# Row maxima of attention from rounded q and k alone, two tiles of queries at once in the lower and upper 64 rows

## What is computed

```python
qkv = jnp.einsum('bte,fe->btf', x, Wqkv)          # split in q, k, v for 8 heads of 64
q = q + pe[None, None]
k = k + pe[None, None]
scores = jnp.einsum('bhtd,bhsd->bhts', q, k) / jnp.sqrt(jnp.asarray(D, q.dtype))
scores = jnp.where(causal[None, None], scores, jnp.asarray(-jnp.inf, q.dtype))
probs = jax.nn.softmax(scores, axis=-1)
attn = jnp.einsum('bhts,bhsd->bhtd', probs, v)
```

## Time and profile before

| | us |
|---|---|
| runs of the kernel | 678.23, 680.35, 681.81 (median 680.35) |
| span of the profiled execution | 680.5 |
| TensorE busy | 629.8 (93%) |
| VectorE busy | 513.4 (75%) |
| GpSimd busy | 505.5 (74%) |
| ScalarE busy | 442.2 (65%) |
| score pairs of the fifth head start at | 273.89 |
| score pairs of the sixth head start at | 330.62 |

### The profile page before, as it was taken

The page is one execution under the profiler, slowest core; times in us unless marked ns, Lnnn a source line. Parts: engine busy times, 40 slices in busy tenths (PEclk is TensorE's granted clock), DMA queues, the critical chain, the costliest instruction groups (busy, mean ns, idle before and its releaser), DMA issues. The chain is left out here.

```text
span 680.5 us, 9930 instructions
## 1 busy us (share of the span) xinstructions
PE 629.8 (93%) x3043; PEld 485.0 (71%) x3043; DVE 513.4 (75%) x1138; ACT 442.2 (65%) x617; POOL 505.5 (74%) x296
## 2 busy tenths in 40 slices
PE   5879999999999999999999999999966998989992
PEld 3647777777777777777777777777655896767761
DVE  3676888887977888888797788886778774785675
ACT  3536786676776668667677666867843666656671
POOL 8016898887888889898788888989986545466770
PEclk8988999999999999999999999999987998999997
DMA  7622322223322232222332223333000000000001
GB/s 200 140 47 48 79 62 47 47 47 70 71 47 46 48 78 63 48 47 47 69 71 47 47 48 70 70 88 116 0 1 0 2 1 1 0 17 0 15 0 31
DMA packets 29074, 33.72 MB, mean 50 GB/s; under 512 B 6977, under 2 KB 15970, under 8 KB 28898
## 3 DMA queue, kind: packets, MB, share of 16 engines
q1 hardware_dynamic: 29026, 33.14, 20.2%
HBM read 6.84 MB, written 1.05 MB: 12 GB/s over the span
## 5 line engine op out<-in xcount | busy, mean ns | idle before, releaser
L391 POOL TENSOR_TENSOR probs_l<-probs,probs_h 128x1024 fp32r<-128x1024 f32 (+1 forms) x160 | 348.2, 2190 | 96.3 <-ACT probs_h L438 49.7
L435 ACT ACTIVATE probs<-scores 128x1024 f32<-128x1024 f32 (+1 forms) x160 | 150.5, 941 | 117.7 <-PE scores L658 61.6
L690 PE MATMUL out_ps<-probs_h,v 128*128 128x512 f32 (+5 forms) x640 | 181.3, 367 | 2.3 <-POOL probs_l L391 1.8
L517 DVE TENSOR_REDUCE m_part<-max_ps 128x1 f32<-128x512 f32 x192 | 127.0, 682 | 51.3 <-PE max_ps L631 50.0
L438 ACT ACTIVATE probs_h<-scores 128x1024 fp32r<-128x1024 f32 (+1 forms) x160 | 149.9, 937 | 0.0
L1037 POOL TENSOR_TENSOR v<-hid,k 128x512 fp32r<-128x512 f32 x64 | 83.3, 1308 | 58.2 <-ACT k L1113 45.2
L657 PE MATMUL scores<-q,k 128*128 128x512 f32 (+1 forms) x320 | 123.1, 385 | 0.0
L690 PEld LDWEIGHTS out_ps<-probs_h,v 128*128 128x128 f32 (+1 forms) x640 | 97.6, 162 | 28.3 <-POOL probs_l L391 7.2
L658 PE MATMUL scores<-q,k 128*128 128x512 f32 (+1 forms) x320 | 117.5, 367 | 0.0
L690 PE MATMUL out_ps<-probs_l,v 128*128 128x512 f32 (+1 forms) x320 | 116.9, 365 | 0.0
L631 PE MATMUL max_ps<-k,q 128*128 128x512 f32 (+2 forms) x320 | 104.1, 399 | 10.1 <-DVE m_part L517 8.1
(11 more groups left out here) (230 smaller groups left out, 986.8 us busy)
## 6 DMA issues: line engine op xcount, KB each, us to landing
k<-qk SPq DMA_DIRECT2D x96, 128.0 KB, 2.3
q<-qk SPq DMA_DIRECT2D x96, 128.0 KB, 2.3
q<-m_turn SPq DMA_DIRECT2D x128, 0.5 KB
v_all<-L_ffn_ew SPq DMA_DIRECT2D x2, 768.0 KB, 8.1
probs<-L_attn_x SPq DMA_DIRECT2D x4, 256.0 KB, 4.3
pos<-positions SPq DMA_DIRECT2D x1, 1024.0 KB, 6.0
out<-v_all SPq DMA_DIRECT2D x4, 256.0 KB, 2.3
acc<-L_attn_Wqkv SPq DMA_DIRECT2D x6, 128.0 KB, 3.1
```

The lines of the kernel that those rows point to most:

```text
L391: pool.tensor_tensor(probs_l[:, p % 2, :, lo:CH], probs[:, p % 2, :, lo:CH], probs_h[:, n % 3, :, lo:CH], ALU.subtract).then_inc(S["probs_ ...
L435: act.activation(probs[:, p % 2, :, lo:CH], scores[:, p % 2, :, lo:CH], ACT.Exp, scale=D ** -0.5).then_inc(S["probs_ready"], 1)
L517: dve.tensor_reduce(m_part[:, r, 2 + j:3 + j], max_ps[:, u % 2, :], AX.X, ALU.max).then_inc(S["tile_max_ready"], 1)
L690: last = pe.matmul(o_ps(h, c)[0:rows, lo:CH], v, pr, start=(p == PAIR0[c] and j == 0 and k == 0), stop=(p == PAIR0[c + 1] - 1 and j == 1 a ...
```

## The change

q's parts are laid in `q1` by tile: tiles 0 and 2 of a chunk keep hi below and lo above, tiles 1 and 3 have hi in the upper 64 rows and lo in the lower. The scores are the same sum, as `k1` is alike in both halves. For that SP moves q hi and q lo in two DMAs each, of two tiles of 128 columns. The maximum uses hi of q and hi of k alone: 64 rows a tile. One tile of an even number (rows 0 to 63, bank 0) and the next one (rows 64 to 127, bank 1) form a pair, one pair a slot; TensorE signals once behind the second, and waits once, for VectorE's release of the whole pair before. VectorE reduces a full pair in one operation over both banks; on the diagonal it reduces each tile's rest by itself and masks both tiles in one addition.

```diff
 def units(p, h):
-    for n in (2 * p + LEAD, 2 * p + LEAD + 1):
-        of, u = (h, n) if n < NU else (h + 1, n - NU)
-        if 0 <= of < H:
-            yield of, u
+    n = 2 * p + LEAD
+    of, u = (h, n) if n < NU else (h + 1, n - NU)
+    if 0 <= of < H:
+        yield of, u
+def both_place(u):
     c = chunk_of(UNIT0, u)
-    r, j = divmod(u - UNIT0[c], c + 1)
-    return c, r, j, (CH if j < c else P * (r + 1))
+    half, j = divmod((u - UNIT0[c]) // 2, c + 1)
+    return c, 2 * half, j
+def tiles_of(a, odd):
+    return a.rearrange("p (t s q) -> p t s q", s=2, q=P)[:, :, odd, :]
...
-                        move(q1[0:D, qs], qk_hi[0:D, :], max_moved)
+                        for odd in range(2):
+                            move(tiles_of(q1[odd * D:(odd + 1) * D, qs], odd), tiles_of(qk_hi[0:D, :], odd), max_moved)
                         sp.wait_ge(S["qk_low_ready"], of * NC + c + 1)
-                        move(q1[D:P, qs], qk_lo[0:D, :], max_moved)
+                        for odd in range(2):
+                            move(tiles_of(q1[(1 - odd) * D:(2 - odd) * D, qs], odd), tiles_of(qk_lo[0:D, :], odd), max_moved)
...
-                        dve.wait_ge(S["max_scores_ready"], of * NU + u + 1)
+                        dve.wait_ge(S["max_scores_ready"], (of * NU + u) // 2 + 1)
                         if j < c:
-                            dve.tensor_reduce(m_part[:, r, 2 + j:3 + j], max_ps[:, u % 2, :], AX.X, ALU.max).then_inc(S["tile_max_ready"], 1)
-                        elif r == 0:
-                            dve.tensor_tensor(m_diag[:, r, :], max_ps[:, u % 2, 0:P], mask_qk[:], ALU.add).then_inc(S["tile_max_ready"], 1)
+                            dve.tensor_reduce(m_part[:, r:r + 2, 2 + j], max_ps[:], AX.X, ALU.max).then_inc(S["tile_max_ready"], 1)
                         else:
-                            dve.tensor_tensor(m_diag[:, r, :], max_ps[:, u % 2, width - P:width], mask_qk[:], ALU.add)
-                            dve.tensor_reduce(m_part[:, r, 1:2], max_ps[:, u % 2, 0:width - P], AX.X, ALU.max).then_inc(S["tile_max_ready"], 1)
+                            pieces = max_ps[:].rearrange("p b (n e) -> p (b n) e", e=P)
+                            if r:
+                                dve.tensor_reduce(m_part[:, r, 1:2], max_ps[:, 0, 0:r * P], AX.X, ALU.max)
+                            dve.tensor_reduce(m_part[:, r + 1, 1:2], max_ps[:, 1, 0:(r + 1) * P], AX.X, ALU.max)
+                            own = pieces[:, r:r + TPC + 2:TPC + 1, :]
+                            dve.tensor_tensor(m_diag[:, r:r + 2, :], own, mask_qk[:].unsqueeze(1).to_broadcast([P, 2, P]), ALU.add).then_inc(S["tile_max_ready"], 1)
...
-            def maximum(h, u):
+            def maxima(h, u):
...
-                wait(pe, S["tile_max_ready"], h * NU + u - 1)
-                n = max(width, 2 * P)
-                ks = slice(j * CH, j * CH + n)
-                tile = q_place(h, c) + r * P
-                last = pe.matmul(max_ps[:, u % 2, 0:n], q1[:, tile:tile + P], k1[:, h % 2, ks], start=True, stop=True)
+                wait(pe, S["tile_max_ready"], (h * NU + u) // 2)
+                for odd in range(2):
+                    n = CH if j < c else max((r + odd + 1) * P, 2 * P)
+                    rows = slice(odd * D, (odd + 1) * D)
+                    tile = q_place(h, c) + (r + odd) * P
+                    last = pe.matmul(max_ps[:, odd, 0:n], q1[rows, tile:tile + P], k1[rows, h % 2, j * CH:j * CH + n], start=True, stop=True)
                 last.then_inc(S["max_scores_ready"], 1)
```

More of the change, by code:

```diff
@@ L34 @@
 LEAD = 22
+MAX_MOVES = 6
 PAIRS = [2 * (c + 1) for c in range(NC)]
@@ L161, in units @@
 def units(p, h):
-    for n in (2 * p + LEAD, 2 * p + LEAD + 1):
-        of, u = (h, n) if n < NU else (h + 1, n - NU)
-        if 0 <= of < H:
-            yield of, u
-def unit_place(u):
+    n = 2 * p + LEAD
[3 more added lines that the diff above has]
+def both_place(u):
     c = chunk_of(UNIT0, u)
-    r, j = divmod(u - UNIT0[c], c + 1)
-    return c, r, j, (CH if j < c else P * (r + 1))
+    half, j = divmod((u - UNIT0[c]) // 2, c + 1)
+    return c, 2 * half, j
 def bank_in_turn(h, c):
@@ L330, in section @@
                         c = chunk_of(UNIT0, u)
-                        if u + 1 == UNIT0[c + 1]:
+                        if u + 2 == UNIT0[c + 1]:
                             sp.wait_ge(S["row_max_turned"], of * NC + c + 1)
@@ L338, in section @@
                         sp.wait_ge(S["qk_positioned"], H * NC)
-                        sp.wait_ge(S[f"max_operands_moved_{n % 2}"], moves(n, 4))
+                        sp.wait_ge(S[f"max_operands_moved_{n % 2}"], moves(n, MAX_MOVES))
                         sp.wait_ge(S[f"score_operands_moved_{n % 2}"], moves(n, 2))
@@ L346, in _ @@
                 section(h)
-            sp.wait_ge(S[f"max_operands_moved_{(H * NC - 1) % 2}"], moves(H * NC - 1, 4))
+            sp.wait_ge(S[f"max_operands_moved_{(H * NC - 1) % 2}"], moves(H * NC - 1, MAX_MOVES))
             sp.wait_ge(S[f"score_operands_moved_{(H * NC - 1) % 2}"], moves(H * NC - 1, 2))
@@ L424, in section @@
                         if n >= 2:
-                            act.wait_ge(S[f"max_operands_moved_{n % 2}"], moves(n - 2, 4))
+                            act.wait_ge(S[f"max_operands_moved_{n % 2}"], moves(n - 2, MAX_MOVES))
                             act.wait_ge(S[f"score_operands_moved_{n % 2}"], moves(n - 2, 2))
@@ L498, in section @@
                         if n >= 2:
-                            dve.wait_ge(S[f"max_operands_moved_{n % 2}"], moves(n - 2, 4))
+                            dve.wait_ge(S[f"max_operands_moved_{n % 2}"], moves(n - 2, MAX_MOVES))
                             dve.wait_ge(S[f"score_operands_moved_{n % 2}"], moves(n - 2, 2))
@@ L511, in section @@
                     for of, u in units(p, h):
-                        c, r, j, width = unit_place(u)
+                        c, r, j = both_place(u)
                         if u == UNIT0[c]:
                             wait(dve, S["row_max_ready"], of * NC + c)
-                        dve.wait_ge(S["max_scores_ready"], of * NU + u + 1)
+                        dve.wait_ge(S["max_scores_ready"], (of * NU + u) // 2 + 1)
                         if j < c:
-                            dve.tensor_reduce(m_part[:, r, 2 + j:3 + j], max_ps[:, u % 2, :], AX.X, ALU.max).then_inc(S["tile_max_ready"], 1)
-                        elif r == 0:
-                            dve.tensor_tensor(m_diag[:, r, :], max_ps[:, u % 2, 0:P], mask_qk[:], ALU.add).then_inc(S["tile_max_ready"], 1)
-                        else:
-                            dve.tensor_tensor(m_diag[:, r, :], max_ps[:, u % 2, width - P:width], mask_qk[:], ALU.add)
-                            dve.tensor_reduce(m_part[:, r, 1:2], max_ps[:, u % 2, 0:width - P], AX.X, ALU.max).then_inc(S["tile_max_ready"], 1)
-                        if u + 1 == UNIT0[c + 1]:
+                            dve.tensor_reduce(m_part[:, r:r + 2, 2 + j], max_ps[:], AX.X, ALU.max).then_inc(S["tile_max_ready"], 1)
+                        else:
+                            pieces = max_ps[:].rearrange("p b (n e) -> p (b n) e", e=P)
[4 more added lines that the diff above has]
+                            dve.tensor_tensor(m_diag[:, r:r + 2, :], own, mask_qk[:].unsqueeze(1).to_broadcast([P, 2, P]), ALU.add).then_inc(S["tile_max_ready"], 1)
+                        if u + 2 == UNIT0[c + 1]:
                             n = of * NC + c
-                            dve.wait_ge(S["tile_max_ready"], of * NU + u + 1)
+                            dve.wait_ge(S["tile_max_ready"], (of * NU + u) // 2 + 1)
                             dve.tensor_reduce(m_part[:, :, 0], m_diag[:], AX.X, ALU.max).then_inc(S["diagonal_max_ready"], 1)
@@ L620, in project @@
                 last.then_inc(S["qk_projected"], 1)
-            def maximum(h, u):
-                c, r, j, width = unit_place(u)
+            def maxima(h, u):
+                c, r, j = both_place(u)
                 if u == UNIT0[c]:
                     n = h * NC + c
-                    pe.wait_ge(S[f"max_operands_moved_{n % 2}"], moves(n, 4))
-                wait(pe, S["tile_max_ready"], h * NU + u - 1)
-                n = max(width, 2 * P)
-                ks = slice(j * CH, j * CH + n)
-                tile = q_place(h, c) + r * P
-                last = pe.matmul(max_ps[:, u % 2, 0:n], q1[:, tile:tile + P], k1[:, h % 2, ks], start=True, stop=True)
+                    pe.wait_ge(S[f"max_operands_moved_{n % 2}"], moves(n, MAX_MOVES))
+                wait(pe, S["tile_max_ready"], (h * NU + u) // 2)
[4 more added lines that the diff above has]
+                    last = pe.matmul(max_ps[:, odd, 0:n], q1[rows, tile:tile + P], k1[rows, h % 2, j * CH:j * CH + n], start=True, stop=True)
                 last.then_inc(S["max_scores_ready"], 1)
@@ L698, in section @@
                     for of, u in units(p, h):
-                        maximum(of, u)
```

(3 more changed lines are left out.)

## The result

The changed kernel takes 706.75 us (median of four runs, 704.70 to 707.56) against 680.70 of the kernel before beside it; the ratio is 1.0381, 95% interval 1.0355 to 1.0406. It is slower, by what the likeliest case of the prediction gave (704.5, 694 to 714).

A forecast was written before the change was run, and what follows sets the result against it. TensorE's stream was taken to set the pace; heads 0 to 6 at 3.1 us each (21.7), last head 1.3 and set-up 1.1 make 24, so 680.5 + 24 = 704.5 us, likeliest case 694 to 714, overall range 660 to 716.

The forecast's parts named there:

- the likeliest case of the prediction: Whole kernel: passage paid and halves side by side, 704.5 us (694 to 714), chance 0.58.
- Passage, 0.35 a pair: TensorE, each slot: going from 128-row matmuls to 64-row ones and back costs 0.35 us, zero being the other end.
- Shift of the second half, 0.06: TensorE, within a pair: the second half starts later by its own weight load, 0 to 0.12 us, middle 0.06 taken.
- One of the signs: TensorE timeline: if right, 0.6 to 0.7 us pass from the last score matmul to the first L690.
- A head: +3.1 forecast: Middle head: +4.1 us raw from the pairs on TensorE, 1.0 taken back as hidden, so +3.1 (1.9 to 4.3).
- the 0.5 put on them: TensorE's waits for GpSimd or VectorE elsewhere: the later stream takes them in, about 0.5 us a head.
- the masks, which were to hide 0.7: Eight causal-mask slots: the pair's extra 0.09 us from an open weight load falls inside the passage, 0.7 a head.
- Set-up, +1.1 forecast: Set-up section: eleven pairs cost about 2.2 us, other waits hide half, leaving 1.1.
- No passage: Rival on TensorE: 64 rows behave as 64 columns do, halves run together, 662 us (651 to 671), chance 0.24.
- Halves in a row: Rival on TensorE: passage paid, halves one after the other, 0.81 us a full pair, 727 us, chance 0.10.
- Nothing on TensorE: Rival: no passage, halves in a row; only the joint wait, 0.2 to 0.7 a head, about 683 us, chance 0.08.
- The moves, put at nothing: SP's q1 DMAs, four instead of two a chunk: later moves 1.25 us late, costing nothing while the three-slot lead stands.

The follow-up runs named there:

- The four shapes: Kernel before plus one unused 256-column matmul a slot: 64 rows 744.80 us, 128 rows 690.86, 128 rows with 64 weight columns 691.48, 32 rows 745.80.
- the control: Kernel before plus one unused matmul a slot ahead of the maxima, 128 rows, 128 columns of weights, 256 moving columns: 690.86 us.
- after with VectorE's units first: Changed kernel with VectorE's joint reduction in slot 1 put ahead of the lo part of q and k: 703.29 us, ratio to before 1.0329.
- the run with both in the lower rows: Changed kernel with both matmuls of a pair in the lower 64 rows, queries from q2, also waiting for q2's moves: 740.58 us, ratio 1.0893.
- full rows: Changed kernel with both matmuls of a pair using all 128 rows; joint wait, joint reduction and six moves kept: 689.92 us against 679.91, ratio 1.0150.
- the two kernels with VectorE's units first: Changed kernel with 128-row pairs (685.85 us) and changed kernel with 64-row pairs (703.29 us), both with slot 1's reduction ahead of the lo part.

## Why the prediction was right

The mechanism was the forecast one, a price for going to 64 rows and back that exceeds what side by side saves. That the sum came so close is in part luck, as several errors cancelled.

**Passage, 0.35 a pair: right in kind, 0.40 in size.** The step rested on L716, one matmul, against 320 narrow ones at L690, and it took the single row because it has fewer rows, like the change. The four shapes show that this was the right ground: 64 and 32 rows pay, 64 columns don't. The Trainium skill's rule ("TensorEngine Tiling (Array Packing)", Key Properties: a change of tiling mode drains the engine) agrees with the run for rows; for columns the run of 691.48 against the control's 690.86 speaks against it.

**Shift of the second half, 0.06: mis-sized; it is 0.003 to 0.004.** The 0.12 at its upper end was that of two loads into the same rows. The Trainium skill's figure ("TensorE: Matmul & The Clock Gate", Part 3: some 4 ns between matmuls in different row groups) agrees with the 3 or 4 ns between the starts in the trace. The two errors cancel by luck: 0.40 + 0.23 = 0.63 for a full pair where the sum had 0.64, and 0.52 where it had 0.53.

One of the signs was no sign: "from the last score matmul to the first L690 passes 0.6 to 0.7 us" is what before has already, to whatever product comes next (0.64 and 0.70 in slots 6 and 14 of the fifth head). After has 0.75 in both, as 0.11 of the passage falls behind that next matmul. The weight loads and the starts of the halves decided.

**A head: +3.1 forecast, +2.9 measured.** With the measured pairs the raw cost is 12 x 0.17 + 4 x 0.28 + 4 x 0.18 = 3.9; 1.0 of it is hidden, as forecast, but not where it was looked for. The eight masked slots grew by 1.1 together, the others by 1.8. Slot 2, which was to lose 0.2, lost nothing; slots 4 and 5 grew by 0.02 each and slot 15 is 0.17 shorter. In slots 4, 5 and 15 it had been 0.62, 0.73 and 0.91 in before from the last score or mask matmul to the next product, longer than a stream without waits, and is 0.52, 0.65 and 0.76 now (in slot 4 the pair also has other widths). In slots 4 and 5 the second unit came late behind VectorE; in slot 15 it was GpSimd's subtraction that the product waited for, in before:

```profile
317.26 0.73 PE L690 MATMUL out_ps<-probs_h,v 128*128 128x512 f32 x2
```

The trace puts 0.5 us of idle time of its weight load down to GpSimd's `probs_l` (L391). In after the product follows the pair by 0.43, as in the slots without a wait. By the columns of each slot's own matmuls, which lie partly in other slots than before, some 0.95 is hidden in slots 2, 4, 5 and 15 (an estimate from 0.40 and the pitches; reckoned so, the raw cost is 4.1 and 1.2 is hidden), and 0.2 in the six other masked slots together. So it was waits that the later stream took in, about twice the 0.5 put on them, and the masks, which were to hide 0.7, hid little: two sizes that were wrong and cancelled.

The first head grew by 2.0 alone, for the reason given under the table, so that seven heads make 19.1 in the traces where the sum had 21.7.

**Last head: +1.3 forecast, +1.3 measured.**

**Set-up, +1.1 forecast, +3.2 in this trace: mis-sized, and only in part explained.** The code of the set-up is the same in after and in after with VectorE's units first, and there the first score matmul starts at 46.2, not 48.0. Windows of after and of that kernel:

```profile
30.00:35.00 5.00, 5.00 (x13) 2.75 (x13) 2.49 (x6) 1.19 (x2) 0.00 (x0) 0.50 0.52 121
```

```profile
30.00:35.00 5.00, 4.22 (x18) 2.22 (x17) 3.61 (x6) 1.64 (x3) 0.00 (x0) 1.00 0.45 104
```

At clock 0.50 (1.2 GHz) TensorE gets through 13 matmuls in 5 us, at 1.00 through 18. So some 1.8 of the 3.2 go with the clock of this one execution. The other 1.4 stay open between the moves, the passage and the clock: from 40 to 45 us the kernel with the units first is granted 0.52 and before 0.91, and the run with the moves alone, at half clock there too, starts nearly as late (46.0).

**The base.** The prediction read the span of 680.5 as a time. The runs show 1.7 to 3.2 between the two, mostly about 2.0 (706.37 and 704.4), so that the profiled execution of before was about 682.5 long, an estimate, and a long one of its kernel: in the runs beside the experiments its spans are 675.5 to 681.0. Against the spans the forecast was 24 and 23.9 were found, which is luck: the heads were put 2.6 too high, and the set-up and the end 2.4 too low. Between the medians the loss is 26.0, and the forecast 2.0 short.

**The rivals.** No passage: falls by the weight loads at 305.86 and 306.29. Halves in a row: falls by the starts of the two halves and by the run with both in the lower rows, 3.6 us a head above. Nothing on TensorE: its condition isn't met, and its price was wrong as well: the run that is that case (full rows) took 689.9, not 683. The step that failed there was "0.2 to 0.7 a head" for the joint wait, counted for slot 2 alone; it is 0.9 a head, and the first score matmul started 3.5 later.

**VectorE.** 1.22 forecast, 1.219 measured; the saving is worth nothing while TensorE sets the pace.

**The moves, put at nothing.** The run with the moves alone bears this out within its interval (680.85 against 679.91, ratio 0.9997 to 1.0035).

## What to carry to other kernels

Half-height matmuls side by side save a pitch a pair (0.23 us here, for 512 columns), and going to them and back costs 0.40 us: one pair between full-height matmuls loses 0.17. By these numbers, as an estimate, two pairs in a row would come out about even (0.46 saved against 0.40) and more of them ahead, which was not tried. Look for the price in the weight loads: a load that no longer starts with the matmul before is the sign of it, and the distance from the last matmul before to the second one behind gives the sum. A joint wait saves instructions on the engine that waits less, and holds both buffers until the longer operation ends; before merging, look at what the first release lets start, and at whether the order in front of it can be changed instead, which here was worth 5.9 us for a few lines (0.6 a middle head; in the first head the clock of one execution had a part).

## What the runs showed that was not expected

A change of weight columns (128 to 64 and back) shows no cost (691.48 us against the control's 690.86, one run of each) where a change of rows costs 0.40 us, and 32 rows cost as much as 64 (745.8 and 744.8). The expectations of these runs had both; nothing in before but one matmul of 21 rows told the two apart.

In the set-up section the half-height pairs help against full-height pairs with the same joint wait. There TensorE and VectorE wait for each other in turn; at half clock the pair of full rows and that of half rows read, in the two kernels with VectorE's units first (TensorE, then VectorE's reduction):

```profile
44.90 1.22 PE L649 MATMUL max_ps<-k,q 128*128 128x512 f32 x2 [0.71 <-DVE m_diag L537]
46.15 1.23 DVE L530 TENSOR_REDUCE m_part<-max_ps 128x2 f32<-128x1024 f32 x1 [1.31 <-PE max_ps L649]
```

```profile
43.38 0.79 PE L649 MATMUL max_ps<-k,q 64*128 64x512 f32 x2 [0.72 <-DVE m_diag L537]
44.21 1.23 DVE L530 TENSOR_REDUCE m_part<-max_ps 128x2 f32<-128x1024 f32 x1 [0.89 <-PE max_ps L649]
```

VectorE waits 0.42 less for this pair, and the first score matmul starts at 46.2 against 48.5. From 45 to 50 us both executions are granted 0.50, from 40 to 45 us 0.52 and 0.59.

The clock in the set-up differs between executions of the same code: 0.50 from 30 to 35 us in after, 1.00 in the kernel with the same set-up. What decided it is open; TensorE had been busy 2.76 and 2.72 of the 5 us before.
